# A graph layer's softmax: the mask made and added during the scores, the exponential in two parts

## The reference, cut to what matters

```python
scores = jax.nn.leaky_relu(hmid @ A2 + b2, SLOPE)
w = jax.nn.softmax(scores.mean(axis=-1), axis=0)
out = jax.ops.segment_sum(w[:, None] * v[tgt], src, num_segments=num_nodes)
y = h + out
```

## Time and profile before

| what | value |
|---|---|
| median of 3 runs | 6014.7 us (6012.15 to 6015.27) |
| the profiled execution | 6016.62 us |
| its span in the profile | 6014.8 us |
| PE busy | 4941.3 us, 82% of the span |
| DVE busy | 4273.0 us, 71% |
| ACT busy | 2873.8 us, 48% |
| POOL busy | 3193.9 us, 53% |
| stage of leftover scores | from 4245 to 5087 us |
| junction, from the last scores to the first sum on PE | from 5087 to 5110 us |
| stage of sums | from 5110 to 6008 us |

### The profile page before, as it was taken

How to read it: one execution, slowest core, us unless ns; L and a number is a source line. 1 busy time by engine, 2 the same in 40 slices (tenths; PEclk the granted TensorE clock), 3 DMA queues, 4 the chain that set the end, 5 groups by cost and what they waited for, 6 DMA issues and landing times. The chain is left out here.

```text
span 6014.8 us, 147634 instructions
## 1 busy us (share of the span) xinstructions
PE 4941.3 (82%) x37917; PEld 3835.8 (64%) x37917; DVE 4273.0 (71%) x11290; ACT 2873.8 (48%) x6430; POOL 3193.9 (53%) x3405
## 2 busy tenths in 40 slices
PE   7656666666666669999999999998799998999999
PEld 4545455545555556666666666666466665999998
DVE  7544444444444458878887887887688888899999
ACT  5333333333333335555555555554244444788887
POOL 2777777777777777777777777777100000000000
PEclk9877888888888889999999999999899999999999
DMA  7877656666564457666766666665566564999999
GB/s 216 243 251 250 205 171 199 197 198 200 198 199 161 142 173 208 204 204 203 206 203 203 205 204 201 206 204 175 140 148 148 149 148 122 263 275 274 275 276 257
DMA packets 1770277, 1218.41 MB, mean 203 GB/s; under 512 B 622292, under 2 KB 1640528, under 8 KB 1770211
## 3 DMA queue, kind: packets, MB, share of 16 engines
q1 hardware_dynamic: 1601393, 762.08, 49.4%
q0 software_dynamic: 154752, 449.19, 20.5%
q10 hardware_dynamic: 14066, 6.41, 0.4%
HBM read 629.52 MB, written 587.74 MB: 202 GB/s over the span
## 5 line engine op out<-in xcount | busy, mean ns | idle before, releaser
L1051 POOL DMA_INDIRECT slots<-rows,slot_i x3224 | 3106.5, 964 | 996.8 <-issue 954.4
L1103 PE MATMUL ps_row<-win,mixed 128*128 128x256 f32 x6448 | 1892.0, 427 | 755.5 <-ACT rows L1182 755.4
L1103 PEld LDWEIGHTS ps_row<-win,mixed 128*128 128x128 f32 x6448 | 1277.4, 214 | 961.0 <-ACT rows L1182 794.0
L1182 ACT ACTIVATE rows<-ps_row 128x512 f32<-128x512 f32 x1612 | 936.1, 596 | 652.9 <-PE ps_row L1103 639.3
L836 ACT ACTIVATE low<-ps_z 128x512 f32<-128x512 f32 x882 | 526.6, 597 | 1113.9 <-PE ps_z L717 627.0
L1826 PE MATMUL ps_y<-v_rows,spot 128*128 128x128 f32 x7056 | 872.7, 281 | 48.4 <-ACT spot L1948 44.7
L1826 PEld LDWEIGHTS ps_y<-v_rows,spot 128*128 128x128 f32 x7056 | 831.2, 192 | 89.8 <-DVE spot L2093 54.3
L2093 DVE TENSOR_SCALAR spot<-iota_f,v_rows,weight 128x128 f32<-128x128 f32 x2646 | 751.5, 345 | 58.5 <-DMA v_rows<-slots 36.5
L853 DVE TENSOR_SCALAR onehot<-ps_lo,part 128x512 bf16<-128x512 f32 x882 | 658.8, 747 | 184.7 <-PE ps_s L789 122.9
L862 DVE TENSOR_TENSOR mid<-low,ps_z 128x512 f32<-128x512 f32 x882 | 599.8, 680 | 200.7 <-ACT low L836 200.7
L717 PE MATMUL ps_z<-onehot,q_bits 128*128 128x512 bf16 (+1 forms) x2940 | 736.5, 366 | 1.6 <-DVE q_bits L751 1.6
(11 more groups left out here) (169 smaller groups left out, 5383.2 us busy)
## 6 DMA issues: line engine op xcount, KB each, us to landing
u_rows<-slots SPq DMA_DIRECT2D x882, 258.0 KB, 2.9
v_rows<-slots SPq DMA_DIRECT2D x784, 258.0 KB, 3.9
slots<-no_row SPq DMA_DIRECT2D x202, 544.0 KB, 3.2
edges<-edge_attr_dram SPq DMA_DIRECT2D x403, 256.0 KB
slots<-rows,slot_i POOLq DMA_INDIRECT x3224
win<-kv_tab SPq DMA_DIRECT2D x403, 64.0 KB
v_rows<-slots SPq DMA_DIRECT2D x196, 129.0 KB, 3.4
q_rows<-q_tab SPq DMA_DIRECT2D x196, 64.0 KB, 2.4
```

Source lines behind the costliest of these rows:

```text
L1051: pool.indirect_dma_start(slots_tab[h], bass.IndirectOffsetOnAxis(slot_i[:, u, j:j + 1], 0), rows[:, u, j, :], None).then_inc(scattered[u] ...
L1103: last = pe.matmul(ps_row[:, k % 2, j % 2, :], mixed[:, u % 2, j, :], win[:, u, :], start=True, stop=True)
L1182: nc.scalar.activation(rows[:, u, 2 * k:2 * k + 2, 0:2 * U0].rearrange("p j (a c) -> p j a c", a=2)[:, :, :, 0:D], ps_row[:, k % 2, :, :]. ...
```

## The change

The mask of piece 1 is made at the start of the third block (`find_inside(1)`, `make_mask(1)`), and `take_scores` of the leftover scores adds it while it takes a pass's 36 columns out of PSUM. The mask of piece 0 is made in pass 0 of the leftover scores (`k` = 6 and 8), and added to its finished scores and reduced in pass 48 (`k` = 2 and 6). After the last scores DVE reduces piece 1 alone and takes the larger of the two tops. ACT raises one element right after its last `raised`, then the exponential of the first `SOON` = 8 tiles, and that of the other 90 after its first three units of `spot`; their negatives go the same way. DVE makes `spot` once the first part is raised; the two totals are spread, added and inverted in step 6 of the sums.

```diff
+SOON = 8
...
         def take_scores(dve, o, i):
 
 
+            at = bass.ds(i * CHUNKS + o.h * HELD, CHUNKS)
             dve.wait_ge(o.sum_made, sum_count(o, i, PU - 1))
-            nc.vector.tensor_copy(score[:, bass.ds(i * CHUNKS + o.h * HELD, CHUNKS)], o.ps_sum[:, P:P + CHUNKS]).then_inc(o.scored, 1)
+            if o.h == 0:
+                nc.vector.tensor_copy(score[:, at], o.ps_sum[:, P:P + CHUNKS]).then_inc(o.scored, 1)
+            else:
+                dve.wait_ge(mask_chain, 2)
+                nc.vector.tensor_tensor(score[:, at], o.ps_sum[:, P:P + CHUNKS], weight[:, at], ALU.add).then_inc(o.scored, 1)
...
-                    pool.wait_ge(mask_chain, 4)
+                    pool.wait_ge(top_found, 3)
                     nc.gpsimd.partition_all_reduce(top_all[:], top[:], P, RMAX).then_inc(top_spread, 1)
-                    pool.wait_ge(exp_ready, 1)
+                    pool.wait_ge(exp_ready, 2)
                     nc.gpsimd.partition_all_reduce(total_all[:], total[:], P, RADD).then_inc(sum_spread, 1)
...
+                def part_of(table, n):
+
+                    b0, b1 = ((0, SOON), (SOON, NT))[n]
+                    return table[:].rearrange("p (h q) -> p h q", h=PIECES)[:, :, b0 * PART:b1 * PART]
+
+                def raise_weights(n):
+
+                    nc.scalar.activation(part_of(weight, n), part_of(score, n), ACT.Exp, bias=shift[:, 0:1], scale=1.0 / H,
+                                         accum_out=total[:, n:n + 1]).then_inc(exp_ready, 1)
+
+                def negate_weights(n):
+
+                    nc.scalar.mul(part_of(minus, n), part_of(weight, n), -1.0).then_inc(minus_ready, 1)
...
                 def sum_step(i, k):
                     if has(i, k + BUNCH):
                         place_last(*unit_at(i, k + BUNCH))
+                    if known(i) and i == 0 and k == BUNCH:
+                        act.wait_ge(exp_ready, 2)
+                        negate_weights(1)
+                    if known(i) and i == 0 and k == 2 * BUNCH:
+                        act.wait_ge(minus_ready, 2)
...
                     raise_heads(act, o, NP - 1, PU - 1)
+                    nc.scalar.activation(ready_exp[:], eps[:], ACT.Exp)
                     act.wait_ge(top_spread, 1)
                     nc.scalar.mul(shift[:], top_all[:], -1.0 / H).then_inc(shifted, 1)
                     act.wait_ge(shifted, 1)
-                    nc.scalar.activation(weight[:], score[:], ACT.Exp, bias=shift[:, 0:1], scale=1.0 / H, accum_out=total[:]
-                                         ).then_inc(exp_ready, 1)
+                    raise_weights(0)
                     act.wait_ge(exp_ready, 1)
-                    nc.scalar.mul(minus[:], weight[:], -1.0).then_inc(minus_ready, 1)
+                    negate_weights(0)
                     act.wait_ge(minus_ready, 1)
                     for k in range(BUNCH):
                         place_last(0, k)
+                    raise_weights(1)
                     unit_steps(act, sum_step)
...
+                    mask_on_the_way(i, k)
                     if k == 5 and past_pair(i, -PU):
                         take_scores(dve, o, i - 1)
...
-                def mask_scores():
...
-                    dve.wait_ge(o.scored, NP)
...
-                    op.then_inc(mask_chain, 1)
-                    dve.wait_ge(mask_chain, 1)
-                    nc.vector.tensor_scalar(weight[:], inside[:], 3e38, -3e38, ALU.mult, ALU.add).then_inc(mask_chain, 1)
-                    dve.wait_ge(mask_chain, 2)
-                    nc.vector.tensor_tensor(score[:], score[:], weight[:], ALU.add).then_inc(mask_chain, 1)
-                    dve.wait_ge(mask_chain, 3)
-                    nc.vector.tensor_reduce(top[:], score[:], AX_X, ALU.max).then_inc(mask_chain, 1)
+                def held_of(h):
+                    return slice(h * HELD, (h + 1) * HELD)
+
+                def find_inside(h):
+
+                    nc.vector.tensor_tensor(inside[:, held_of(h)].rearrange("p (t c) -> p t c", c=PART),
+                                            slot_of[:].rearrange("p (a c) -> p a c", a=1).to_broadcast([P, NT, PART]),
+                                            cnt[:, 0:NT, h].rearrange("p (t a) -> p t a", a=1).to_broadcast([P, NT, PART]),
+                                            ALU.is_lt).then_inc(mask_chain, 1)
+
+                def make_mask(h):
+
+                    dve.wait_ge(mask_chain, 1 + 2 * (1 - h))
+                    nc.vector.tensor_scalar(weight[:, held_of(h)], inside[:, held_of(h)], 3e38, -3e38, ALU.mult, ALU.add
+                                            ).then_inc(mask_chain, 1)
+
+                def mask_first():
+
+                    dve.wait_ge(mask_chain, 4)
+                    nc.vector.tensor_tensor(score[:, held_of(0)], score[:, held_of(0)], weight[:, held_of(0)], ALU.add
+                                            ).then_inc(mask_chain, 1)
+
+                def find_top(h):
+
+                    if h == 0:
+                        dve.wait_ge(mask_chain, 5)
+                    else:
+                        dve.wait_ge(o.scored, NP)
+                    nc.vector.tensor_reduce(tops[:, h:h + 1], score[:, held_of(h)], AX_X, ALU.max).then_inc(top_found, 1)
+
+                def mask_on_the_way(i, k):
+
+                    if known(i) and i == 0 and k == 6:
+                        find_inside(0)
+                    if known(i) and i == 0 and k == 8:
+                        make_mask(0)
+                    if known(i) and i == NP - 1 and k == 2:
+                        mask_first()
+                    if known(i) and i == NP - 1 and k == 6:
+                        find_top(0)
...
+                def invert_total():
+
+                    dve.wait_ge(sum_spread, 1)
+                    nc.vector.tensor_tensor(total_all[:, 0:1], total_all[:, 0:1], total_all[:, 1:2], ALU.add).then_inc(divisor, 1)
+                    dve.wait_ge(divisor, 1)
+                    nc.vector.reciprocal(inv[:], total_all[:, 0:1]).then_inc(divisor, 1)
+                    dve.wait_ge(divisor, 2)
+
                 def sum_step(i, k):
                     if has(i, k + BUNCH):
                         place(*unit_at(i, k + BUNCH))
+                    if known(i) and i == 0 and k == 2 * BUNCH:
+                        dve.wait_ge(exp_ready, 2)
+                        invert_total()
...
                 def with_slots():
+                    find_inside(1)
+                    make_mask(1)
...
                     take_scores(dve, o, NP - 1)
-                    mask_scores()
-                    dve.wait_ge(sum_spread, 1)
-                    nc.vector.reciprocal(inv[:], total_all[:]).then_inc(divisor, 1)
-                    dve.wait_ge(divisor, 1)
+                    find_top(1)
+                    dve.wait_ge(top_found, 2)
+                    nc.vector.tensor_tensor(top[:], tops[:, 0:1], tops[:, 1:2], ALU.max).then_inc(top_found, 1)
+                    dve.wait_ge(exp_ready, 1)
                     for k in range(BUNCH):
                         place(0, k)
```

More of the change, by code:

```diff
@@ L1502, in gnn_layer @@
             inside = tmp("inside", [P, NT * CHUNKS])
+            tops = tmp("tops", [P, PIECES])
             top = tmp("top", [P, 1])
@@ L1505, in gnn_layer @@
             shift = tmp("shift", [P, 1])
-            total = tmp("total", [P, 1])
-            total_all = tmp("total_all", [P, 1])
+            total = tmp("total", [P, 2])
+            total_all = tmp("total_all", [P, 2])
+            ready_exp = tmp("ready_exp", [P, 1])
             inv = tmp("inv", [P, 1])
@@ L1541, in gnn_layer @@
         mask_chain = sem("mask_chain")
+        top_found = sem("top_found")
         top_spread = sem("top_spread")
```

5 lines of the change are left out of this document (removed).

## The result

| what | kernel before | changed kernel |
|---|---|---|
| median of the runs | 6015.05 us (6011.77 to 6017.96, 14 runs) | 6000.56 us (5996.44 to 6005.72, 14 runs) |
| ratio to before, 95% interval | | 0.9976 [0.9967, 0.9984] |
| the profiled execution | 6016.62 us | 6002.87 us |
| its span in the profile | 6014.8 us | 6001.0 us |

The changed kernel is 14.5 us faster, where 13.5 were forecast. To see where the time went I cut each span in five: up to the third block's first load on SP, from there to the end of the last `take_scores`, from there to PE's first sum, to PE's last sum, and the rest. Each bound is the start or end of one row of the timeline.

A forecast was written before the change was run, and what follows sets the result against it. PE was taken to bound scores and sums, with a serial chain of 23.4 us between them; 18.0 - 3.0 - 1.5 = 13.5 us gained gave 6001.2 us, range 5997.0 to 6006.0.

The forecast's parts named there:

- The junction: Between last scores and first sum, where PE stands still: 23.4 us falls to about 5.4, 18.0 us gained.
- The insertions: Piece 0's mask operations in the first and last score passes: PE loses 1.14, 0.55 and 1.32, reduce covered; 3.0 us lost.
- The mask of piece 1 at the start: Third block's start, ahead of the first `lo_b`: 3.1 us fits into DVE's 3.7 us wait for rows, cost 0.
- The masked take: `take_scores` in the score loop becomes an add over 36 columns: same 0.20 us, 0.52 of room, 49 takes cost nothing.
- The ramp: Start of the sums: ACT's late large operations make PE wait for unit 7; 1.5 us lost, bounds 0 and 6.0.
- insertions covered: Rival in the score loop: later steps regain the inserted mask time; gain 16.5, time 5998.2 us, chance 0.15.
- ACT paid whole: Rival in the sums: ACT's late work costs 6.0 instead of 1.5; gain 9.0, time 6005.7 us, chance 0.15.
- it doesn't do what it says: Rival at the junction: the early table load still delays `shift`, 1.3 + 0.2 us; time 6002.7 us, chance 0.03.
- Slower: Rival in the score loop: the masked take runs beyond its 0.52 of cover; at 1.3 us more, 6038 us; chance 0.02.
- The clock falls back: Rival in the sums: PE's pause before unit 7 brings back half clock; 2.6 us, time 6003.8 us, chance 0.13.

The follow-up runs named there:

- one exponential: Changed kernel with one exponential and one negative over 3528 columns ahead of the first spot: 7444.75 us on a slower chip, ratio to before 0.9985.
- the second profile: The changed kernel once more, word for word, on another chip: median 6000.92 us, ratio to before 0.9977; profile span 5999.1 us.
- the longer operations: Changed kernel with an extra DVE add behind each pass's take, over 256 or 1024 columns: 6002.69 and 6042.83 us.
- the long operation: Changed kernel with an extra DVE add over 1024 columns behind each pass's take: 6042.83 us beside 6014.65 before.
- the table load at the junction: Changed kernel without the one-element exponential, so the table loads at the first real exponential: 7446.35 us on a slower chip, ratio to before 0.9986.
- the kernel with the mask on POOL: Changed kernel with piece 0's mask made and added on POOL at the third block's start: 7443.9 us on a slower chip, ratio to before 1.0000.
- both operations in a row: Changed kernel with the large negative straight behind the large exponential on ACT: 6003.55 us, ratio to before 0.9981.

## Why the prediction was right

The time was forecast at 6001.2 and is 6000.56, and the terms hold up one by one, save that of the ramp.

- **The junction:** 18.0 forecast, 18.16 measured. From the last scores to the sums it is 5.21 us, forecast 5.4. By experiment 5.4 of it is the split (one exponential: 10.62) and 1.28 the table load, forecast 1.3. The Trainium skill (ScalarE: Activation LUTs, What ACT_TABLE_LOAD costs) gives about 2.66 us for a switch; row and run both say 1.28.
- **The insertions:** forecast 1.14, 0.55 and 1.32 and a free reduce, sum 3.0. Measured 1.13, 0.37 and 1.32 and nothing (between the last two takes, where the reduce stands, it is 7.45 us before and after), sum 2.82. The stage grew by 2.75 us in the second profile and by 1.73 in the first, whose first take came 1.0 us earlier after the block's first load than in the second profile (40.45 against 41.40).
- **The mask of piece 1 at the start:** forecast hidden, and it is. `weight` ends at 4249.54, `lo_b` begins at 4250.19 and waits for the load, not for DVE:

```profile
4246.43 2.00 DVE L2107 TENSOR_TENSOR inside<-slot_of,cnt 128x1764 f32<-128x1764 f32 x1 [43.47 <-PEq L961]
...
4248.46 1.08 DVE L2115 TENSOR_SCALAR weight<-inside 128x1764 f32<-128x1764 f32 x1
...
4250.19 0.17 DVE L851 CAST lo_b<-u_rows 128x4 bf16<-128x4 f32 x1 [0.65 <-DMA u_rows<-slots]
```

- **The masked take:** forecast 0.20 us with 0.52 of cover. It takes 0.193 where the copy took 0.186, and the pass stays at 16.92. The result was right and the cover too large: the slack that counted is not the idle time ahead of the next `onehot` but what is left at that step's `lo_b`, which the earlier trace rows showed as 0.22 ahead of PE for another step, and which the longer operations put at 0.35 here. The point from which the change loses moves down from 0.81 us to (13.5 + 0.35 x 47) / 47 = 0.64 us more per take. With the measured 14.5 for 13.5, the long operation should make the kernel 47 x (1.215 - 0.35) - 14.5 = 26 us slower than the one before; it was 28.
- **The ramp:** forecast a pause of about 2.5 us before unit 7 until +11.6, unit 17 at +21.7, the stage 1.5 us longer. Measured 2.32 us, +11.57, +21.54 (+21.84 in the second profile). In this, two errors ahead of unit 3 cancelled: the clock rose after 3.6 us and not 6, so PE was done with unit 2 at +4.63 and not +5.3, and then the large exponential was not hidden, for PE waited 0.81 us and began unit 3 at +5.44. ACT sets the later times, and its part was right to two tenths. Yet the stage is only 0.27 and 0.01 us longer. **This is the term that was mis-sized:** I took unit 17 for the end. At unit 17 the changed kernel is 1.3 us behind the one before, at unit 50 1.0, at unit 300 0.9, at unit 600 and unit 881 0.3; the second profile has 1.6, 1.3, 1.2, 0.2 and 0.0. So most of it is made good behind unit 300. That the late start is gone at the end is measured. Why is not: kernels without the pause have sums of 896.6 to 898.5 us, those with it and at full clock 897.4 to 898.7, and within this spread the pause has no price. I can't tell whether later loads or DVE's waits give it back.
- **What the sum left out:** the rest behind PE's last sum is 0.8 us longer in both profiles. It is no term of the change: among the ten other kernels, which all have the same end, it lasts from 7.1 to 8.7 us. It and the ramp's 1.2 to 1.5 have opposite signs, and both are smaller than the spread of the part ahead of the change, so that the total came within 0.7 us is in part luck.

Of the rivals, *insertions covered* fell (their waits are in the rows), *ACT paid whole* fell (1.3 and not 6.0 at unit 17), *it doesn't do what it says* fell (the table load is hidden). *Slower* has its mechanism shown at the longer extra operation and was far off. *The clock falls back* deserves more than its place: it did not happen in either profile of the changed kernel, but did in two kernels next to it. Its price was put at 2.6 us. With the table load at the junction it is 1.6 us at unit 10 and 1.7 at unit 50, against the kernel with the mask on POOL, which has the same pause on the same chip; the rest of the 4.4 by which those sums are longer came later. With both operations in a row it is 4.0 with the longer pause in it. The runs of the changed kernel spread from 5996.4 to 6005.7 us. Those of the kernel before, which has no such pause, spread from 6009.2 to 6019.5, and the changed kernel's eleven later ones show no steps of 4 us, so the spread doesn't need the clock. Whether some of them have the half clock behind the pause can't be seen without a trace of each, and stays open.

## What to carry to other kernels

Where every engine waits in one serial chain, each link can be priced from its own row, and here the sum of the links held to tenths of a microsecond. Work moved out of it into a stage that one engine bounds costs its duration less the slack at that place. That slack is found by following the step to the operand that the bounding engine takes last. A late start of a long streaming stage is not yet a late end: carry it through the stage, or give it a range down to zero. And before work goes to an idle engine or into an idle time, look at who works beside it: the same mask cost 2.8 us between the steps, 7.7 on POOL (849.79 against 842.11 without it), and by the rows 2.9 in an idle stretch of DVE.

## What the runs showed of the hardware that was not expected

- DVE is slowed severely beside POOL's work on f32 tiles in SBUF: from 2.00 to 5.00 us and from 1.08 to 2.42 us, and even copies of four columns waited, three taking 4.64 us. Two of POOL's indirect transfers took 2.40 and 2.44 us instead of 0.96 beside DVE's operations over 1764 columns (two with two inputs and one with one), and one took 0.96 beside a reduce.
- Around a pause of PE of 2.32 us the granted clock stayed full in five profiles and was half for 3.4 us in a sixth, with the same work around it; there it fell 0.7 us after PE had gone on. Around a pause of 3.42 us it was half for 6.8 us.
- The clock rose 3.6 us after the first sum in the changed kernel and 6.0 us after it in the kernel before. With the table load at the junction it was 5.4, in the ten other profiles 2.9 to 5.0, 4.1 in the second of the changed kernel. The length of the idle time ahead does not order these: the shortest, 2.9, stands behind the longer junction of 10.62 us.
